# Two-layer token kernel: the first stage's preparation of a tile moved from one to three tiles ahead

## The chip, the cores and the metric

One core of a Trainium2 chip runs the kernel; all inputs and outputs lie in its memory. The metric is the device time of one execution in microseconds (us), lower is better.

## The reference, cut to what matters

`x` is [32, 64, 1024] in float32, 2048 tokens of 1024 features (32 batches of 64 channels).

```python
x = x + ffn0(cond0(x, cond_128))      # first stage
x = x + ffn1(cond1(x, cond_128))      # second stage
# cond0: a weighted mix of eight 64x64 kernels for each batch
att = softmax(mlp(cond_128))                      # [32, 8]
y = einsum('boi,bih->boh', einsum('bk,koi->boi', att, weight), x) + (att @ bias_k)[:, :, None]
# ffn0: eight experts that scale inputs and outputs of one product with the signs of W
routing = softmax(y @ gate_w.T)                   # [2048, 8]
out = (y * (routing @ in_scale)) @ sign(W).T * (routing @ out_scale) + bias
# cond1: grouped convolution over the features; ffn1: dense product plus gated low-rank experts
```

## The kernel before, in words

The 2048 tokens are 16 tiles of 128 tokens (two batches each), in pairs: tile t is written `(i, p)` with t = 2i + p. Two stages follow one another. The first computes x1 = x + ffn0(cond0(x)) tile by tile and stores x1 in a scratch tensor; the second reads x1 back and computes the output. The change is in the first stage, its start and its hand-over to the second.

Five engines have their programs written out by hand, each in its own order, tied by semaphores.

**TensorE** (PE). For tile t of the first stage it makes `product_y` (L375 to L384: the 128x128 block-diagonal mixing matrix `agg` of two batches against x, eight float32 matmuls, 16 records, L382), `product_logits` (L386 to L393: eight matmuls with y as the stationary operand and eight moving columns, 16 records, L391), `turn_routing` (a transpose, L397), `product_scales` (L399 to L412: eight 32-row matmuls and two 32-row ones of 512 columns, L405 and L411), and the signed product `ffn0_step`, 32 matmuls of 128x512 (L429) into two banks. A period (`period0`, L442) is the signed product of one tile with the preparation of the next one set in: y ahead of it, logits at step 12, the transpose at 20, scales at 26.

**VectorE** (DVE) adds the mixing bias to y (L748), makes the next mixing matrix (`mix_kernels`, L719 and L724), takes part in the softmax (L755, L757, L762), scales y to u (`scale_in`, L769), makes the low part of u (`take_rest`, L776), and scales the product (`scale_out`, L784). **ScalarE** (ACT) takes the signs at the start (L586), makes the exponentials (L593), spreads and rounds the routing (L598, L604), rounds u (L609), copies the out-scales from the bank to `os_sb` (`copy_out_scale`, L620, which waits for POOL to be done with the tile before), and rounds one chunk of the second stage's weights per pair (L624).

**GpSimd** (POOL) makes x + bias in one of two buffers `resid` (`add_bias0`, L891), reading x from `xs`; then x1 from it, half by half (`make_x1`, L899); and once per pair the low part of a chunk of weights (`rest_of_stage`, L903). Its order for a pair: x1 of tile (i,0), a chunk, bias of (i+1,0), x1 of (i,1), bias of (i+1,1). The bias add waits until x1 of the tile two before is stored, since it writes the same buffer.

**SyncE** (SP) issues nearly all transfers, in program order and waiting in line: for a pair x of the next pair (L222), the bias row of the tile (L227), the store of x1 (L263), a chunk of weights (L230). At the hand-over it issues the 16 loads of the second stage's first two tiles (`load_raw`, L303) behind the store of tile 13. In the second stage it stores an output tile, waits for the landing, and reloads x1 into the same buffer (L327, L318); POOL adds a bias to it (L931).

The second stage is 16 periods of L491 (its dense products), L473 (the convolution) and L519. Its first product waits for the low parts of u's successor z (L776), and for `rest_of_stage` of the eighth chunk.

## Time and profile before

| | us |
|---|---|
| median of 3 runs | 585.76 (585.52 to 588.63) |
| the profiled execution's own time | 585.94 |
| its span | 584.2 |
| PE busy | 569.8 (98%) |
| DVE busy | 232.6 (40%) |
| POOL busy | 148.1 (25%) |
| ACT busy | 118.9 (20%) |
| first stage's steady periods, from the span's start | 38.4 to 204.2 |
| second stage begins | 215.0 |

A timeline row gives start and duration in us, the engine, the line of the kernel, the operation, what it writes and reads, how many instructions are merged in it, and in brackets the idle time before it and what ended that. In a row of PE the duration is from the first start to the last end, and a matmul of 0.4 us overlaps the next one, so a group's cost is read from start to start, or from the chain of waits, whose pieces do not overlap. A row of a transfer gives its issue; the time from issue to landing stands in the rows of its line. A name such as `work` stands for both `resid` and `os_sb`, which are parts of it.

### The profile page before, as it was taken

What the parts mean: (1) busy time and instruction counts of PE and PEld (TensorE: products, weight loads), DVE (VectorE), ACT (ScalarE), POOL (GpSimd) and SP (SyncE); (2) the same over time, 40 slices, a digit from 0 to 9 for tenths busy, and PEclk for the clock granted to TensorE, in tenths of its full rate; (3) what the DMA queues carried; (4) which work ended last, traced back from release to release, by engine and by line L of the source; (5) the groups of instructions that cost most, each with busy time, mean ns of one, the idle gap of its engine ahead of it and who ended that gap; (6) DMA issues with size and microseconds to landing.
All of it is one profiled execution on the core that took longest, in us unless ns stands there. A gap on an engine that the chain in (4) does not pass through costs nothing.

```text
span 584.2 us, 9131 instructions
## 1 busy us (share of the span) xinstructions
PE 569.8 (98%) x3381; PEld 502.3 (86%) x3381; DVE 232.6 (40%) x446; ACT 118.9 (20%) x271; POOL 148.1 (25%) x79
## 2 busy tenths in 40 slices
PE   4799999999999999999999999999999999999997
PEld 3688888888888899989989889899899898898996
DVE  3675677557765555221232232222312322222121
ACT  4732333324233341011111011011110110100100
POOL 0425636555456456101011011011010110110100
PEclk9889999999999999999999999999999999999999
DMA  8905324443253664303203123033032130230100
GB/s 327 356 34 162 117 78 132 135 119 117 76 175 100 158 165 123 111 3 113 90 24 112 45 67 112 33 79 103 9 112 75 37 112 36 76 111 8 67 37 36
DMA packets 36175, 58.16 MB, mean 100 GB/s; under 512 B 4097, under 2 KB 24385, under 8 KB 36161
## 3 DMA queue, kind: packets, MB, share of 16 engines
q1 hardware_dynamic: 36016, 57.70, 31.9%
q10 hardware_dynamic: 144, 0.26, 0.1%
q8 instruction: 10, 0.16, 0.1%
q14 instruction: 5, 0.03, 0.0%
HBM read 41.15 MB, written 16.79 MB: 99 GB/s over the span
## 4 chain that ended last, share of the span: by engine, by line
PE 94%; DVE 0%; issue 0%
PE bank L491 49%; PE bank L429 21%; PE bank L473 10%; PE bank L391 4%; PE bank L382 4%; PE bank L519 4%; PE bank L405 1%; PE bank L397 0%; PE bank L512 0%; PE bank L411 0%; DVE work L748 0%; DVE work L874 0%
## 5 line engine op out<-in xcount | busy, mean ns | idle before, releaser
L491 PE MATMUL bank<-early,parts 128*128 128x320 f32 (+1 forms) x1152 | 206.5, 337 | 0.0
L491 PEld LDWEIGHTS bank<-early,parts 128*128 128x128 f32 x1152 | 184.7, 188 | 15.7
L429 PE MATMUL bank<-late,parts 128*128 128x512 f32 x512 | 134.5, 411 | 1.5 <-ACT parts L609 1.5
L429 PEld LDWEIGHTS bank<-late,parts 128*128 128x128 f32 x512 | 93.5, 193 | 21.9 <-ACT parts L609 1.9
L931 POOL TENSOR_TENSOR work<-work,bias_bc 128x1024 f32<-128x1024 f32 x16 | 38.7, 2424 | 286.5 <-DMA work<-x_scratch 286.5
L491 PE MATMUL bank<-late,parts 128*128 128x512 f32 x384 | 94.2, 394 | 0.0
L491 PEld LDWEIGHTS bank<-late,parts 128*128 128x128 f32 x384 | 70.9, 188 | 16.1
L473 PE MATMUL bank<-band,raw 128*128 128x128 f32 x512 | 59.7, 275 | 0.0
L473 PEld LDWEIGHTS bank<-band,raw 128*128 128x128 f32 x512 | 59.0, 192 | 0.1
L609 ACT ACTIVATE parts<-work 128x512 fp32r<-128x512 f32 x64 | 39.8, 632 | 80.3 <-DVE work L823 43.0
L899 POOL TENSOR_TENSOR work<-work 128x512 f32<-128x512 f32 x32 | 41.3, 1291 | 52.5 <-DVE work L784 52.5
L776 DVE TENSOR_TENSOR parts<-work,parts 128x512 fp32r<-128x512 f32 x64 | 46.8, 753 | 12.2 <-ACT parts L609 10.6
L891 POOL TENSOR_TENSOR work<-xs,bias_bc 128x1024 f32<-128x1024 f32 x16 | 38.7, 2424 | 45.3 <-DMA x_scratch<-work 23.1
L845 DVE TENSOR_TENSOR qk<-bank,qk 128x256 f32<-128x256 f32 x16 | 6.8, 424 | 100.5 <-ACT qk L666 100.5
L864 DVE TENSOR_TENSOR wh_t<-bank,wh_t 128x128 fp32r<-128x128 f32 x16 | 4.7, 292 | 95.0 <-ACT wh_t L674 95.0
L874 DVE TENSOR_TENSOR work<-bank,work 128x512 f32<-128x512 f32 x32 | 22.1, 692 | 50.7 <-PE bank L519 50.7
L382 PEld LDWEIGHTS bank<-agg,xs 128*128 128x128 f32 x256 | 32.5, 200 | 1.4 <-issue 0.2
L391 PEld LDWEIGHTS bank<-cst,work 128*128 128x128 f32 x256 | 31.4, 194 | 2.0 <-issue 0.9
L382 PE MATMUL bank<-agg,xs 128*128 128x128 f32 x256 | 33.0, 285 | 0.0
L391 PE MATMUL bank<-cst,work 128*128 128x8 f32 x256 | 30.1, 253 | 0.5 <-DVE work L748 0.5
L664 ACT ACTIVATE qk<-bank 128x64 f32<-128x64 f32 x16 | 3.6, 225 | 119.0 <-PE bank L491 119.0
L519 PE MATMUL bank<-lora,wh_t 128*128 128x512 f32 x96 | 27.6, 396 | 0.0
(88 smaller groups left out, 344.4 us busy)
## 6 DMA issues: line engine op xcount, KB each, us to landing
xs<-in_x SPq DMA_DIRECT2D x16, 512.0 KB, 3.9
x_scratch<-work SPq DMA_DIRECT2D x16, 512.0 KB, 3.0
raw<-x_scratch SPq DMA_DIRECT2D x128, 64.0 KB, 3.0
work<-x_scratch SPq DMA_DIRECT2D x16, 512.0 KB, 3.6
out_tokens<-work SPq DMA_DIRECT2D x15, 512.0 KB, 2.7
stage<-in_wearly SPq DMA_DIRECT2D x8, 576.0 KB, 3.8
row_bc<-token_rows_scratch SPq DMA_DIRECT2D x30, 64.0 KB, 3.6
work<-in_wsign SPq DMA_DIRECT2D x3, 512.0 KB, 11.3
```

The costliest lines, as they stand in the source:

```text
L382: last = mm(bank[h][:, c * P:(c + 1) * P], xs[:, p, at:at + P], agg[:, p, :], start=True, stop=True)
L391: last = mm(bank[2][:, 0:E], y_t[:, c, :], cst[:, C_GATE + c * E:C_GATE + (c + 1) * E], start=(c == 0), stop=(c == L8 - 1))
L429: last = mm(bank[4 + h][:, :], parts[:, p, a, c, :], signs[:, c, h * HALF:(h + 1) * HALF], start=(k % 16 == 0), stop=(k % 16 == 15))
L473: last = mm(bank[n // 4][:, (n % 4) * P:(n % 4 + 1) * P], raw[:, p, n, s:s + P], band[:, s * GROUPS + n % 4, :], start=(s == 0), stop=(s = ...
L491: return mm(dst, parts[:, p, a, c, :], w(b, c), start=(k == 0), stop=(close and k == 23))
L519: last = mm(o[h][:, :], wh_t[:, a, :], lora[:, b, h * HALF:(h + 1) * HALF], start=False, stop=(k == 2))
L609: do(cols(parts[:, p, 0], h), cols(y_t, h), ACT.Copy).then_inc(done, 1)
L776: v.tensor_tensor(cols(parts[:, p, 1], h), cols(y_t, h), cols(parts[:, p, 0], h).bitcast(F32), ALU.subtract).then_inc(done, 1)
L874: v.tensor_tensor(o, bank[4 + 2 * p + h][:, :], o, ALU.add).then_inc(out_ready, 1)
L891: g.tensor_tensor(resid[:, p, :], xs[:, p, :], bias_bc[:, :], ALU.add).then_inc(xb_ready, 2)
L899: g.tensor_tensor(resid[:, p, cols], os_sb[:, cols], resid[:, p, cols], ALU.add).then_inc(x1_ready, 1)
L931: g.tensor_tensor(resid[:, p, :], resid[:, p, :], bias_bc[:, :], ALU.add).then_inc(resid_ready, 1)
```

## The change

The first stage becomes a pipeline three tiles deep. In the period of tile t (`i, p`), `one` is tile t+1, `two` t+2, `three` t+3.

- `product_y` uses 64x64 quarters of the array: 32 matmuls of 64 rows, 64 stationary columns and 64 moving columns, on `agg` without its zero blocks. It serves tile t+3.
- `product_logits` has the gate weights, padded to 32 columns, as the stationary operand, and y as the moving one, in four column groups of the array; ACT copies the four partial sums (`copy_logits`), and a matmul `sum_logits` with a selection matrix adds them. Logits serve tile t+2; the sum stands at step 26.
- The transpose of the routing stands at step 7. Logits, y and scales stand together at step 18, the scales of tile t+1 last; these wait for the out-scale copies of tile t.
- y has two buffers of its own; `xs` is let go as soon as y is made, so x is loaded three tiles ahead. x is loaded a second time, straight into `resid`, by `load_again`, and POOL adds the bias in place. `load_again` of tile t+1 is issued by SP behind the store of tile t-1 and its landing (`replace_x1`).
- POOL's order becomes, for each tile t: first half of x1(t), bias of t+1, in every second tile a chunk, second half of x1(t).
- `mix_kernels` needs one reduction of 128 partitions in place of two of 64.
- At the start the constants come in three parts, the signs' loads and roundings are in another order, and the first stage's periods 0 and 1 are written out; at the hand-over SP issues `load_raw` of the second stage's first two tiles ahead of the store of tile 13 and the reload for tile 15.

The diff, cut to its core (indentation shortened):

```diff
-LOGITS_AT, TURN_AT, SCALES_AT, CONV0_AT = 12, 20, 26, 8
-SIGNS_FIRST = 6
+TURN_AT, BLOCK_AT, SUM_AT, CONV0_AT = 7, 18, 26, 8
+SIGNS_FIRST = 4
...
-        work = sb("work", [P, 4, H])
+        y_t = sb("y_t", [P, 2, L8, P])
+        work = sb("work", [P, 3, H])
         xs = sb("xs", [P, 2, H])
         raw = sb("raw", [P, 2, NBG, NB])
...
-        agg = sb("agg", [P, 2, P])
+        agg = sb("agg", [P, 2, S])
...
+  def load_next(i, p, biased):
+      sp.wait_ge(y_biased, biased)
+      load_x(i, p)
+      load_row(aggb_row, i, p, aggb_loaded)
+  def load_again(i, p):
+      sp.dma_start(resid[:, p, :], tile_rows(x, 2 * i + p)).then_inc(x_again_loaded[p], 16)
+  sp.wait_ge(rows_stored, 16)
+  load_next(1, 0, 2)
+  for p in range(2):
+      sp.wait_ge(signs_ready, 7 + p)
+      load_again(0, p)
   sp.wait_ge(scale_ready, 1)
   sp.dma_start(bias_bc[:, :], bias0.broadcast_to([P, H])).then_inc(bias0_loaded, 16)
-  sp.wait_ge(tok_rows_ready, 2)
-  sp.dma_start(rows_dram.rearrange("a b s -> b a s"), tok_rows[:, :, :]).then_inc(rows_stored, 16)
+  load_next(1, 1, 4)
...
+  load_stage(1, bm, H)
   load_stage(0, wearly[:, 0, :], NW)
-  sp.wait_ge(signs_ready, 2)
-  load_stage(1, bm, H)
+  load_next(2, 0, 6)
   for k in range(2):
-      sp.wait_ge(signs_ready, 3 + k)
       sp.dma_start(late_raw[:, k, :], late_pairs[k]).then_inc(late_loaded[k], 16)
-  sp.wait_ge(signs_ready, 6)
   sp.dma_start(band[:, :, :].rearrange("p a n -> p (a n)"), toep).then_inc(band_loaded, 16)
...
+  def store_x1(i, p):
+      sp.wait_ge(x1_ready, 4 * i + 2 * p + 2)
       sp.dma_start(tile_rows(x1_dram, 2 * i + p), resid[:, p, :]).then_inc(x1_stored[p], 16)
-  def load_next(i, p, both):
-      sp.wait_ge(xb_ready, both)
-      sp.wait_ge(y_biased, both)
-      load_x(i + 1, p)
-      load_row(aggb_row, i + 1, p, aggb_loaded)
-  with sp.Fori(0, PAIRS - 1) as i:
-      load_next(i, 0, 4 * i + 2)
-      store_x1(i, 0, 4 * i + 2)
-      load_next(i, 1, 4 * i + 4)
+  def replace_x1(i, p):
+      store_x1(i, p)
+      sp.wait_ge(x1_stored[p], 16 * (i + 1))
+      load_again(i + 1, p)
+  def next_chunk(i):
       sp.wait_ge(stage_hi[0], i + 1)
       sp.wait_ge(stage_lo[0], i + 1)
       load_stage(0, wearly[:, bass.ds(i + 1, 1), :].rearrange("p a n -> p (a n)"), NW)
-      store_x1(i, 1, 4 * i + 4)
+  with sp.Fori(0, PAIRS - 3) as i:
+      load_next(i + 2, 1, 4 * i + 8)
+      replace_x1(i, 0)
+      next_chunk(i)
+      load_next(i + 3, 0, 4 * i + 10)
+      replace_x1(i, 1)
+  late_i, last = PAIRS - 3, PAIRS - 1
+  load_next(last, 1, 4 * late_i + 8)
+  replace_x1(late_i, 0)
+  next_chunk(late_i)
+  replace_x1(late_i, 1)
...
+  sp.wait_ge(y_done, 2 * TILES - 2)
+  sp.dma_start(xs[:, 0, :], late_pairs[3]).then_inc(late_loaded[3], 16)
   for p in range(2):
       sp.wait_ge(y_biased, 4 * last + 2 * p + 2)
       load_row(ctx_row, 0, p, ctx_loaded)
+  replace_x1(last - 1, 0)
+  next_chunk(last - 1)
...
   load_raw(0, 0)
   load_raw(0, 1)
+  replace_x1(last - 1, 1)
   sp.wait_ge(xb_ready, 2 * TILES)
   sp.dma_start(bias_bc[:, :], bias1.broadcast_to([P, H])).then_inc(bias1_loaded, 16)
-  sp.dma_start(xs[:, 0, :], late_pairs[3]).then_inc(late_loaded[3], 16)
-  store_x1(last, 0, 4 * last + 2)
-  store_x1(last, 1, 4 * last + 4)
+  store_x1(last, 0)
+  store_x1(last, 1)
...
   def product_y(i, p):
-      pe.wait_ge(x_loaded[p], 16 * (i + 1))
-      pe.wait_ge(agg_ready, 4 * i + 2 * p + 2)
-      for h in range(2):
-          for c in range(4):
-              at = (4 * h + c) * P
-              last = mm(bank[h][:, c * P:(c + 1) * P], xs[:, p, at:at + P],
-                        agg[:, p, :], start=True, stop=True)
-          last.then_inc(y_done, 1)
-  def product_logits(i, p):
       for c in range(L8):
-          if c % 4 == 0:
-              pe.wait_ge(y_biased, 4 * i + 2 * p + 1 + c // 4)
-          last = mm(bank[2][:, 0:E], y_t[:, c, :], cst[:, C_GATE + c * E:C_GATE + (c + 1) * E],
-                    start=(c == 0), stop=(c == L8 - 1))
-      last.then_inc(logits_done, 1)
-  def turn_routing(i, p):
+          for b in range(2):
+              for g in range(2):
+                  at = c * P + g * S
+                  rows = slice(b * S, (b + 1) * S)
+                  made = mm(bank[b][g * S:(g + 1) * S, c * S:(c + 1) * S], xs[rows, p, at:at + S],
+                            agg[rows, p, :], start=True, stop=True)
+              if c == L8 - 1:
+                  made.then_inc(y_done, 1)
+  def product_logits(i, p, first_tile=False):
+      pe.wait_ge(y_biased, 4 * i + 2 * p + 2)
+      if not first_tile:
+          pe.wait_ge(gate_exp, 2 * i + p)
+      for c in range(L8):
+          at = slice(EP * (c % 4), EP * (c % 4) + EP)
+          made = mm(bank[2][at, 0:P], cst[:, C_GATE + c * EP:C_GATE + (c + 1) * EP], y_t[:, p, c, :],
+                    start=(c < 4), stop=(c >= 4))
+      made.then_inc(logits_made, 1)
+  def sum_logits(i, p, first_tile=False):
+      pe.wait_ge(logits_copied, 2 * i + p + 1)
+      if not first_tile:
+          pe.wait_ge(u_ready, 4 * i + 2 * p - 1)
+      mm(bank[2][:, 0:E], logits_t[:, :], cst[:, C_SEL:C_SEL + E], start=True, stop=True).then_inc(logits_done, 1)
...
+  def product_scales(i, p, first_tile=False, copied=1):
       pe.wait_ge(routing_split, 2 * i + p + 1)
+      pe.wait_ge(logits_copied, 2 * i + p + copied)
+      if not first_tile:
+          pe.wait_ge(out_scale_ready, 4 * i + 2 * p)
...
+  def period0(i, p, one, two=None, three=None):
       for k in range(32):
-          if k == LOGITS_AT:
-              pe.wait_ge(u_ready, 4 * i + 2 * p + 2)
-              product_logits(ni, q)
           if k == TURN_AT:
-              turn_routing(ni, q)
-          if k == SCALES_AT:
-              pe.wait_ge(out_scale_ready, 4 * i + 2 * p + 2)
-              product_scales(ni, q)
-          ffn0_step(i, p, k, first_tile)
-  period0(0, 0, 0, 1, True)
-  period0(0, 1, 1, 0)
-  with pe.Fori(1, PAIRS - 1) as i:
-      period0(i, 0, i, 1)
-      period0(i, 1, i + 1, 0)
+              turn_routing(*one)
+          if k == BLOCK_AT:
+              if three:
+                  inputs_of_y(*three)
+              if two:
+                  product_logits(*two)
+              if three:
+                  product_y(*three)
+              product_scales(*one, copied=2 if two else 1)
+          if k == SUM_AT and two:
+              sum_logits(*two)
+          ffn0_step(i, p, k)
+  for k in range(32):
+      if k == 6:
+          pe.wait_ge(u_ready, 1)
+          product_logits(0, 1)
+      if k == 10:
+          inputs_of_y(1, 0)
+          sum_logits(0, 1)
+          product_y(1, 0)
+      if k == 16:
+          turn_routing(0, 1)
+      if k == 22:
+          inputs_of_y(1, 1)
+          product_logits(1, 0)
+          product_y(1, 1)
+          product_scales(0, 1, copied=2)
+      if k == 28:
+          sum_logits(1, 0)
+      ffn0_step(0, 0, k, True)
+  period0(0, 1, (1, 0), (1, 1), (2, 0))
+  with pe.Fori(1, PAIRS - 2) as i:
+      period0(i, 0, (i, 1), (i + 1, 0), (i + 1, 1))
+      period0(i, 1, (i + 1, 0), (i + 1, 1), (i + 2, 0))
   last_i = PAIRS - 1
-  period0(last_i, 0, last_i, 1)
+  period0(last_i - 1, 0, (last_i - 1, 1), (last_i, 0), (last_i, 1))
+  period0(last_i - 1, 1, (last_i, 0), (last_i, 1))
+  period0(last_i, 0, (last_i, 1))
...
+  def copy_logits(i, p):
+      act.wait_ge(logits_made, 2 * i + p + 1)
+      do(logits_t[:, :], bank[2][:, 0:P], ACT.Copy).then_inc(logits_copied, 1)
...
+  def period0(i, p, one, two=None, chunk=None):
+      if one:
+          round_routing(*one)
+      copy_out_scale(i, p, 1)
+      if chunk is not None:
+          round_stage(0, NW, (chunk + 1) * 16, early[:, 0, bass.ds(chunk, 1), :].rearrange("p a n -> p (a n)"))
+      if two:
+          copy_logits(*two)
+      if one:
+          round_u(*one)
+      if two:
+          gate_exps(*two)
+          spread_routing(*two)
+      if one:
+          copy_out_scale(*one, 0)
...
+  period0(last, 0, (last, 1))
+  period0(last, 1, None, None, last)
...
-      for h in range(2):
-          rows = slice(h * S, (h + 1) * S)
-          v.tensor_reduce(agg[rows, p, rows], weighted[rows, :, :], AX.X, ALU.add).then_inc(agg_ready, 1)
+      v.tensor_reduce(agg[:, p, :], weighted[:, :, :], AX.X, ALU.add).then_inc(agg_ready, 1)
...
+  add_mix_bias(0, 0, True)
+  dve.wait_ge(scale_hi, 1)
+  v.scalar_tensor_tensor(scale_w[:, :], bias_bc[:, 0:HALF], cst[:, C_SLO:C_SLO + 1], scale_w[:, :].bitcast(F32),
+                         ALU.mult, ALU.add).then_inc(scale_ready, 1)
+  mix_kernels(0, 1)
+  route_max(0, 0)
+  route_sum(0, 0)
   split_routing(0, 0)
   scale_in(0, 0)
-  take_rest(0, 0, u_hi, u_lo, by_block)
-  period0(0, 0, 0, 1, first=True)
-  period0(0, 1, 1, 0)
-  with dve.Fori(1, PAIRS - 1) as i:
-      period0(i, 0, i, 1)
-      period0(i, 1, i + 1, 0)
+  rest_of_u(0, 0, 0)
+  add_mix_bias(0, 1, True)
+  rest_of_u(0, 0, 1)
+  mix_kernels(1, 0)
+  route_max(0, 1)
+  route_sum(0, 1)
+  mix_kernels(1, 1)
+  add_mix_bias(1, 0)
+  split_routing(0, 1)
+  scale_out(0, 0, 0)
+  scale_in(0, 1)
+  rest_of_u(0, 1, 0)
+  route_max(1, 0)
+  rest_of_u(0, 1, 1)
+  route_sum(1, 0)
+  add_mix_bias(1, 1)
+  mix_kernels(2, 0)
...
+  def period0(i, p, before, one, two=None, three=None, four=None):
+      scale_out(*before, 1)
+      split_routing(*one)
+      if four:
+          mix_kernels(*four)
+      scale_out(i, p, 0)
+      scale_in(*one)
+      rest_of_u(*one, 0)
+      if two:
+          route_max(*two)
+      rest_of_u(*one, 1)
+      if two:
+          route_sum(*two)
+      if three:
+          add_mix_bias(*three)
+  period0(0, 1, (0, 0), (1, 0), (1, 1), (2, 0), (2, 1))
+  with dve.Fori(1, PAIRS - 2) as i:
+      period0(i, 0, (i - 1, 1), (i, 1), (i + 1, 0), (i + 1, 1), (i + 2, 0))
+      period0(i, 1, (i, 0), (i + 1, 0), (i + 1, 1), (i + 2, 0), (i + 2, 1))
   last = PAIRS - 1
-  period0(last, 0, last, 1, False)
+  period0(last - 1, 0, (last - 2, 1), (last - 1, 1), (last, 0), (last, 1))
+  period0(last - 1, 1, (last - 1, 0), (last, 0), (last, 1))
+  period0(last, 0, (last - 1, 1), (last, 1))
+  scale_out(last, 0, 1)
...
-  def add_bias0(i, p, first_tiles=False):
-      pool.wait_ge(x_loaded[p], 16 * (i + 1))
-      if not first_tiles:
-          pool.wait_ge(x1_stored[p], 16 * i)
-      g.tensor_tensor(resid[:, p, :], xs[:, p, :], bias_bc[:, :], ALU.add).then_inc(xb_ready, 2)
-  def make_x1(i, p):
+  def add_bias0(i, p):
+      pool.wait_ge(x_again_loaded[p], 16 * (i + 1))
+      g.tensor_tensor(resid[:, p, :], resid[:, p, :], bias_bc[:, :], ALU.add).then_inc(xb_ready, 2)
+  def make_x1(i, p, h):
       pool.wait_ge(xb_ready, 4 * i + 2 * p + 2)
-      for h in range(2):
-          pool.wait_ge(scaled, 4 * i + 2 * p + h + 1)
-          cols = slice(h * HALF, (h + 1) * HALF)
-          g.tensor_tensor(resid[:, p, cols], os_sb[:, cols], resid[:, p, cols], ALU.add).then_inc(x1_ready, 1)
+      pool.wait_ge(scaled, 4 * i + 2 * p + h + 1)
+      cols = slice(h * HALF, (h + 1) * HALF)
+      g.tensor_tensor(resid[:, p, cols], os_sb[:, cols], resid[:, p, cols], ALU.add).then_inc(x1_ready, 1)
...
-  pool.wait_ge(signs_ready, L8)
+  pool.wait_ge(u_lo, 2)
   pool.wait_ge(bias0_loaded, 16)
-  add_bias0(0, 0, True)
-  add_bias0(0, 1, True)
+  add_bias0(0, 0)
+  def period0(i, p, one, chunk=None):
+      make_x1(i, p, 0)
+      if one:
+          add_bias0(*one)
+      if chunk is not None:
+          hi, lo = (early[:, a, bass.ds(chunk, 1), :].rearrange("p a n -> p (a n)") for a in range(2))
+          rest_of_stage(0, NW, chunk + 1, lo, hi)
+      make_x1(i, p, 1)
+  period0(0, 0, (0, 1))
   rest_of_stage(1, H, 1, lora[:, 1, :], lora[:, 0, :])
   with pool.Fori(0, PAIRS - 1) as i:
-      make_x1(i, 0)
-      chunk = [early[:, a, bass.ds(i, 1), :].rearrange("p a n -> p (a n)") for a in range(2)]
-      rest_of_stage(0, NW, i + 1, chunk[1], chunk[0])
-      add_bias0(i + 1, 0)
-      make_x1(i, 1)
-      add_bias0(i + 1, 1)
+      period0(i, 1, (i + 1, 0), i)
+      period0(i + 1, 0, (i + 1, 1))
   last = PAIRS - 1
-  make_x1(last, 0)
-  rest_of_stage(0, NW, L8, early[:, 1, L8 - 1, :], early[:, 0, L8 - 1, :])
-  make_x1(last, 1)
+  period0(last, 1, None, last)
```

## Rows read from the trace of the kernel before

**Rows 1.** The page: busy time, share of the span and instructions of each engine.

```profile
PE 569.8 (98%) x3381; PEld 502.3 (86%) x3381; DVE 232.6 (40%) x446; ACT 118.9 (20%) x271; POOL 148.1 (25%) x79
```

**Rows 2.** Chain of waits, start, us, what: tile 14's period and the hand-over.

```profile
192.33 1.78 PE bank L382 x16
...
196.85 1.69 PE bank L391 x16
...
202.58 3.56 PE bank L429 x14
206.14 3.57 PE bank L473 x32
209.71 5.46 PE bank L429 x24
```

**Rows 3.** Timeline of PE, the scale products of one period.

```profile
71.64 0.33 PE L405 MATMUL bank<-routing_t,scale_w 32*128 32x128 f32 x2
71.65 0.50 PE L411 MATMUL bank<-scale_w,routing_t 32*128 32x512 f32 x2
```

**Rows 4.** Timeline of POOL, two tiles of the first stage.

```profile
90.80 2.65 POOL L903 TENSOR_TENSOR early<-stage,early 128x1152 f32 x1 [1.96 <-ACT early L624]
93.42 2.39 POOL L891 TENSOR_TENSOR work<-xs,bias_bc 128x1024 f32<-128x1024 f32 x1
...
99.38 1.30 POOL L899 TENSOR_TENSOR work<-work 128x512 f32<-128x512 f32 x1 [2.33 <-DVE work L784]
103.90 2.40 POOL L891 TENSOR_TENSOR work<-xs,bias_bc 128x1024 f32<-128x1024 f32 x1 [3.22 <-DMA x_scratch<-work]
```

**Rows 5.** Timeline around a second-stage reload: DVE, SP and POOL.

```profile
307.55 0.69 DVE L874 TENSOR_TENSOR work<-bank,work 128x512 f32<-128x512 f32 x1 [2.67 <-PE bank L519]
308.43 0.37 SPq L327 DMA_DIRECT2D out_tokens<-work  x1
...
311.11 0.33 SPq L318 DMA_DIRECT2D work<-x_scratch  x1
...
314.50 2.36 POOL L931 TENSOR_TENSOR work<-work,bias_bc 128x1024 f32<-128x1024 f32 x1 [20.09 <-DMA work<-x_scratch]
```

**Rows 6.** Page, transfers by kind: count, KB each, median us from issue to landing.

```profile
xs<-in_x SPq DMA_DIRECT2D x16, 512.0 KB, 3.9
x_scratch<-work SPq DMA_DIRECT2D x16, 512.0 KB, 3.0
...
work<-x_scratch SPq DMA_DIRECT2D x16, 512.0 KB, 3.6
```

**Rows 7.** The store's line L263, over all 16, min/median/max.

```profile
DMA to landing us min/median/max: 2.9/3.0/7.3
```

**Rows 8.** Busy times by stretch: the start at half clock, then the steady periods.

```profile
24.20:27.90 3.70, 3.70 (x10) 2.71 (x11) 3.70 (x2) 2.31 (x4) 3.70 (x3) 0.54 0.97 343
...
38.40:204.20 165.80, 165.80 (x1051) 141.04 (x1050) 106.35 (x194) 54.30 (x120) 87.74 (x49) 1.00 0.40 123
```

**Rows 9.** Timeline of SP, the hand-over to the second stage.

```profile
197.88 7.47 SPq L303 DMA_DIRECT2D raw<-x_scratch  x16
...
205.87 0.43 SPq L313 DMA_DIRECT2D xs<-in_wlate  x1
207.28 10.38 SPq L263 DMA_DIRECT2D x_scratch<-work  x2
```

**Rows 10.** Timeline of DVE at the start.

```profile
22.64 1.29 DVE L769 TENSOR_TENSOR work<-bank,work 128x512 f32<-128x512 f32 x2 [0.75 <-PE bank L405]
24.09 4.21 DVE L776 TENSOR_TENSOR parts<-work,parts 128x512 fp32r<-128x512 f32 x2 [0.16 <-ACT parts L609]
```

**Rows 11.** Timeline of ACT, the hand-over to the second stage.

```profile
207.34 0.60 ACT L620 ACTIVATE work<-bank 128x512 f32<-128x512 f32 x1 [2.29 <-POOL work L899]
207.84 1.16 ACT L624 ACTIVATE early<-stage 128x1152 fp32r<-128x1152 f32 x1
208.89 0.62 ACT L609 ACTIVATE parts<-work 128x512 fp32r<-128x512 f32 x1
```

223 lines of the change are left out of this document (117 added, 106 removed).

## The prediction

> **What bounds the kernel now.** I read the page first, for the shares: PE is busy 98% of the span and no other engine over 40% [rows 1]. Then the chain of waits in order of time, which shows who sets the pace: in the first stage it is PE alone, in periods of 11.845 us, from 38.4 us (tile 1) to 204.2, all of it busy at full clock [rows 8]; the last full one, tile 14's, starts at 192.33, and the next product of its tile 15 runs on to 215.17, where the second stage begins [rows 2]. Last I read POOL, SP and the transfers, which are not on the chain now, because the change re-orders them and makes them wait on one another in a new way.
>
> **PE's part.** A period holds y for 1.78 us and logits for 1.69 [rows 2]; 16 records each, 0.111 us per record. After, y has 64 records of half the columns. If the four quarters of the array work side by side, that is 16 x 0.056 = 0.9 us; if none do, 64 x 0.056 = 3.6. Logits: 16 records of 128 moving columns in four column groups, 4 x 0.111 = 0.45 side by side, 1.78 one by one; the sum adds 2 x 0.111 = 0.22. The nearest row for overlap is the scale products, four matmuls of different row groups that start within 0.01 us [rows 3]; for column groups no row stands. I take overlap for both. No row prices a change of the array's shape by itself; I allow 0.15 us for each of the two more, between nothing and 0.3. PE's period would be 11.85 - 3.47 + 0.9 + 0.45 + 0.22 + 0.3 = 10.25 us, 1.6 less.
>
> **The new chain through POOL.** x + bias was made from `xs`, which had been loaded long before. Now x is loaded again into `resid`, and only after the store of the tile two before has landed there. Follow one round, from the end of the second half of x1(t-1): SP wakes and issues the store; it lands; SP wakes and issues the reload for tile t+1; it lands; POOL adds the bias for t+1; in every second tile it makes the low part of a chunk; and only then, in its program order, the second half of x1(t). That is a loop from one tile to the next, whatever PE does. Its terms:
> - Store, landing, reload, landing. The second stage does exactly this: DVE ends at 308.24, POOL starts at 314.50, 6.26 us [rows 5]. The store there goes to the output; to the scratch tensor it costs more, POOL's end at 100.68 to its restart on the landing at 103.90 is 3.22 [rows 4], against 2.87 (to the reload's issue) there. With 3.39 for reload and landing and 0.1 for SP's wake I take 6.7. Lower end 6.3; upper end 7.1, from a median of 3.9 for a load of x with another transfer beside it [rows 6].
> - Bias 2.40, second half 1.29 [rows 4]: 3.69.
> - Chunk 2.65 in every second tile [rows 4].
> - In the odd tiles SP is held until that chunk is done, 1.29 us before the x1 ends, and then issues the chunk load (576 KB), x (512 KB) and a row ahead of the store. SP's own issues run to about 0.6 us past x1's end, and the 1.1 MB need 3.3 us at the 343 GB/s of the crowded start [rows 8], of which some 1.1 are left when the store is queued. I take 1.7 for both; lower end 0.6; upper end 4.3, since a store behind two 512 KB loads took 7.3 in place of 3.0 us [rows 7, 9]. Five tiles have it, one more 0.7.
>
> So a pair takes 2 x (6.7 + 3.69) + 2.65 + 1.7 = 25.1 us, 12.6 per tile, against 11.85 now and the 10.25 that PE could do. PE is tied to it: the scales of t+1 wait for ACT's out-scale copy of t, which waits for the second half of x1(t-1). PE waits some 2 us a period at step 18. The routing chain (max, exponential, transpose) was moved a period ahead and has slack of several us; the queues of DVE and ACT are in that wait's shadow, as what stands behind the copy on ACT (chunk rounding 1.16, logits copy about 0.3) delays the scales to 2.3 us after x1, and x1(t)'s own product is ready by about 7, before POOL needs it at 9.1.
>
> One more load on that loop has no row in steady state: a DVE instruction with both inputs in SBUF beside a POOL one. At the start two roundings' rests took 4.21 us in place of 1.3 [rows 10], with POOL at work. That is DVE held up; the loop suffers only if POOL is. I take nothing for it, and keep 0.8 a tile (the mixing product) as its upper end. The Trainium skill (SBUF — State Buffer, section on the two separate sides) says that such pairs lock each other out for a whole instruction, whoever is first; by that rule DVE's mixing product could hold POOL once a tile and the sum would be up to 10 us higher. The trace agrees that the lock exists (4.21 us), and shows no case where POOL lost.
>
> **Start.** The signed product of tile 0 starts as before: the same chain of short steps leads to u at 22.64 [rows 10]. But the second half of tile 0's scale-out moved on DVE behind the mixing work of later tiles: from 22.64 it has 22 operations of 512 columns at 0.7 and six small ones, 16.4 us, so 39.0, and x1(0) would end at 40.3 if DVE never waited. It waits for the scales of tile 1, which stand at step 22 of a half-clocked PE; I take 43.5, with 46 as upper end.
>
> **To tile 13.** 13 rounds of 10.39 are 135.1, seven chunks 18.6, the crowding 5 x 1.7 + 0.7 = 9.2: x1(13) is done at 43.5 + 162.9 = 206.4.
>
> **Hand-over.** Ahead of the store of tile 13 SP now has the chunk load and 16 issues of raw loads, 7.47 us [rows 9]. SP is let go 1.3 before x1(13) ends, so the store is issued 7.2 us after it. Then landing 3.2, reload 3.6: 14.0; bias and half of x1(14) 3.7: 17.7. ACT's copy 0.60, the last chunk's rounding 1.16, both roundings of z 1.25 [rows 11]: 20.7. DVE: last rest of z and scale-out of tile 15, 0.7 each: 22.1. POOL: first half of x1(15), 1.29, then the last chunk, 2.65: 26.1 us. Without that chunk the second stage may not begin. PE alone would be there after 15.5 us (1.3 to the end of the scales, 14 + 32 steps of 0.228 and the convolution's 3.57, all [rows 2]), so it idles some 10 us. The second stage begins at 206.4 + 26.1 = 232.5 in place of 215.2: 17.3 later. After a wait PE restarts at half clock (1.2 of 2.4 GHz): in 24.20 to 27.90 ten records took 3.7 us at a mean clock of 0.54 after a wait of PE [rows 8], and ten at full speed take 2.3 (5.46 for 24 in [rows 2]), so 1.5 are lost; with a second spell like it, 3. I take 1.7.
>
> The second stage's instructions and their order are unchanged. **Sum:** 585.94 + 17.3 + 1.7 = 604.9 for the profiled execution, which stands 0.2 from the median: 605.
>
> **Rivals.**
> - PE sets the pace (faster). It needs a loop under 10.25 us: 6.7 would have to be 5.2 or less, after the 3.69 and the mean chunk of 1.33. Against it: no store landed under 2.9 us and the measured round trip is 6.26 [rows 5, 7]. If it holds, 13 periods and a half at 1.6 less: 585.9 - 22 = 564. The Trainium skill (TensorE: Matmul & The Clock Gate, Part 1) gives a floor of about 25 ns from start to start for small matmuls; y would then be an estimated 1.6 in place of 0.9 and this rival 573. Rows 3's starts, four within 0.01 us, speak against it. Chance 0.07.
> - The loop binds, but mildly (no change): round trip 6.2, no crowding, x1(0) at 40.3. Then x1(13) ends at 40.3 + 13 x 9.89 + 18.6 = 187.5, and with the same hand-over the second stage begins at 213.6: 585.9 - 1.6 + 1.7 = 586. Chance 0.06.
> - Column groups don't overlap (slower, by PE): y 3.6 and logits 1.78 in each period, 14.3 us per tile, over the loop's 12.6. Then 14 x 2.5 = 35 later: 621, and the hand-over's gap closes partly. It decides from a PE period above 12.6. Chance 0.07.
> - The forecast, 0.80. Its own range: round trip, crowding and x1(0) at their low ends take off 5, 6 and 3, giving 592 with a small allowance; crowding, lock and clock at the high ends together would add 13, 10 and 2, of which I take about three quarters: 623.
>
> **Numbers.** 605; range 591 to 623, which holds nearly all of the forecast and of the third rival. A difference under 0.5% (2.9 us) can't be told from none. Faster 0.07, same 0.06, slower 0.87.
>
> **What would show it.** Right: chain of waits with POOL's bias add waiting for the reload, store and load of x in turn, periods of 12 to 13 us alternating short and long, PE idle at step 18 behind the out-scale copy; a gap of several us on PE ahead of the second stage; half clock after it. Wrong: PE busy without gaps in the first stage at 10.3 us a tile, or a POOL that waits for DVE rather than for the reload. If the new y and logits stretches last over 3.6 and 1.7 us, the third rival holds. A hand-over gap under 3 us would break my sum's second part.

## The result and the profile after

The changed kernel takes 620.41 us (median of 4 runs, 618.89 to 621.86) against 585.64 (585.13 to 588.63): a ratio of 1.058, 95% interval [1.055, 1.062]. It is slower, as forecast, and within the range of 591 to 623, but near its upper end, 15 us over the forecast of 605. The profiled execution took 618.89 us, its span is 616.9.

The page after, busy times, as in [rows 1], and the forty slices of PE and its clock:

```profile
PE 559.0 (91%) x4181; PEld 483.5 (78%) x4181; DVE 226.3 (37%) x429; ACT 121.8 (20%) x287; POOL 150.7 (24%) x79
...
PE   4697887979779882999999999999999999999997
...
PEclk9799788979797997999999999999999999999999
```

PE is busy 11 us less, in a span 33 us longer. The waits are in the first sixteen slices (15.4 us each), and its clock falls there again and again. So read what it waits for. The chain of waits of the changed kernel, one round of two tiles in the first stage (start, us, what):

```profile
89.83 5.78 DMA x_scratch<-work
...
95.78 3.24 DMA work<-in_x
...
99.49 1.97 issue
101.46 1.28 POOL work L1031
...
102.91 2.64 DMA x_scratch<-work
...
105.72 3.30 DMA work<-in_x
...
109.29 2.22 issue
111.50 3.15 POOL early L1035
```

Not one piece is PE's. Store, reload, POOL's bias add (printed as issue after its start), in the second tile the chunk, the second half of x1, and the store again: the ring of the prediction. In a tile with a chunk the printed chain goes from the chunk to the next store through the three issues of SP that the chunk lets go; they end with the second half of x1, within 0.3 us. POOL's timeline over the same round; L1024 is the bias add, L1035 the chunk, L1031 the halves of x1:

```profile
85.20 2.68 POOL L1035 TENSOR_TENSOR early<-stage,early 128x1152 f32 x1
87.83 1.73 POOL L1031 TENSOR_TENSOR work<-work 128x512 f32<-128x512 f32 x1
89.83 1.27 POOL L1031 TENSOR_TENSOR work<-work 128x512 f32<-128x512 f32 x1 [0.26 <-DVE work L888]
99.15 2.36 POOL L1024 TENSOR_TENSOR work<-work,bias_bc 128x1024 f32<-128x1024 f32 x1 [8.06 <-DMA work<-in_x]
101.46 2.49 POOL L1031 TENSOR_TENSOR work<-work 128x512 f32<-128x512 f32 x2
109.16 2.39 POOL L1024 TENSOR_TENSOR work<-work,bias_bc 128x1024 f32<-128x1024 f32 x1 [5.20 <-DMA work<-in_x]
111.50 3.14 POOL L1035 TENSOR_TENSOR early<-stage,early 128x1152 f32 x1
```

L1031 at 87.83 and the first part of the merged row at 101.46 are second halves. From the end of a second half (89.56) to the next bias add is 9.59 us when a chunk and x stand ahead of the store in the queue, and 6.42 us (102.74 to 109.16) when they don't. SP's timeline shows the three issues ahead of it:

```profile
88.09 0.33 SPq L235 DMA_DIRECT2D stage<-in_wearly  x1
88.71 0.33 SPq L227 DMA_DIRECT2D xs<-in_x  x1
89.22 0.33 SPq L232 DMA_DIRECT2D row_bc<-token_rows_scratch  x1
89.83 0.35 SPq L286 DMA_DIRECT2D x_scratch<-work  x1
95.78 0.33 SPq L265 DMA_DIRECT2D work<-in_x  x1
```

PE in that period: logits (L433), y (L420), then the wait at step 18, and the scales (L462):

```profile
98.96 0.64 PE L433 MATMUL bank<-y_t,cst 128*32 128x128 f32 x16
99.53 1.16 PE L420 MATMUL bank<-agg,xs 64*64 64x64 f32 x64
104.74 0.47 PE L462 MATMUL bank<-routing_t,scale_w 32*128 32x128 f32 x2 [4.04 <-ACT logits_t L672]
```

The new products are as cheap as taken: logits 0.57 us and y about 1.0 from start to start, for 1.69 and 1.78 of [rows 2]. All quarters and column groups work side by side. What they save PE then spends waiting, 4.04 us here. The wait is printed against the logits copy on ACT, but that one stands behind the out-scale copy, which waits for POOL. The granted clock falls to half (1.2 GHz) during this wait, by 103.0, 1.7 us ahead of the restart, and stays there until some 5 us behind it. The row's columns are those of [rows 8], the clock (0.51) is the third from the end:

```profile
103.20:109.70 6.50, 4.96 (x21) 4.10 (x22) 1.98 (x3) 2.66 (x5) 1.30 (x2) 0.51 0.43 161
```

Last the hand-over, PE's timeline, and SP's, which answer to [rows 2, 9]:

```profile
229.41 5.70 PE L486 MATMUL bank<-late,parts 128*128 128x512 f32 x24
246.61 3.59 PE L570 MATMUL bank<-early,parts 128*128 128x320 f32 x14 [11.50 <-POOL early L1035]
```

```profile
218.54 8.48 SPq L335 DMA_DIRECT2D raw<-x_scratch  x16
227.06 0.43 SPq L286 DMA_DIRECT2D x_scratch<-work  x1
230.27 0.35 SPq L265 DMA_DIRECT2D work<-in_x  x1
```

The store of tile 13 is issued 7.8 us after its x1 is done (219.23), behind the issues of 16 raw loads, and PE stands 11.5 us until POOL has made the last chunk.

Where the 32.7 us of span come from, from the end of x1 of tile 0 and of tile 13 (POOL's timeline) and the start of the second stage:

| stretch | before | after | more |
|---|---|---|---|
| to the end of x1(0) | 41.4 | 46.6 | 5.2 |
| 13 rounds to x1(13) | 154.0 (11.85 each) | 172.6 (13.28) | 18.6 |
| x1(13) to the second stage | 19.6 | 27.4 | 7.8 |
| second stage | 369.2 | 370.3 | 1.1 |

### The profile page after: what moved, and what is told of

The parts are those of the page before. It is cut to its first block, busy times and chain, and to the rows that moved or that the text cites. A ratio compares the mean times of both kernels' runs of the same rounds, so it can differ in the third digit from the quotient of the medians.

```text
span 616.9 us, 10810 instructions
## 1 busy us (share of the span) xinstructions
PE 559.0 (91%) x4181; PEld 483.5 (78%) x4181; DVE 226.3 (37%) x429; ACT 121.8 (20%) x287; POOL 150.7 (24%) x79
## 4 chain that ended last, share of the span: by engine, by line
PE 64%; DMA 15%; issue 7%; POOL 6%; SPq 3%; ACT 2%; DVE 2%; POOLq 0%; ACTq 0%; DVEq 0%
PE bank L570 47%; PE bank L552 9%; DMA x_scratch<-work 8%; DMA work<-in_x 7%; POOL early L1035 4%; PE bank L598 4%; PE bank L486 2%; POOL work L1031 2%; SPq L335 1%; PE bank L420 1%; ACT early L706 1%; ACT late L662 0%; DVE work L888 0%; PE bank L433 0%; DVE parts L880 0%
## 5 line engine op out<-in xcount | busy, mean ns | idle before, releaser
L570 PE MATMUL bank<-early,parts 128*128 128x320 f32 (+1 forms) x1152 | 207.9, 339 | 11.5 <-POOL early L1035 11.5
L486 PE MATMUL bank<-late,parts 128*128 128x512 f32 x512 | 141.2, 431 | 1.5 <-ACT parts L692 1.5
L486 PEld LDWEIGHTS bank<-late,parts 128*128 128x128 f32 x512 | 101.7, 207 | 24.8 <-ACT parts L692 1.6
L1066 POOL TENSOR_TENSOR work<-work,bias_bc 128x1024 f32<-128x1024 f32 x16 | 37.7, 2357 | 289.2 <-DMA work<-x_scratch 289.2
L570 PE MATMUL bank<-late,parts 128*128 128x512 f32 x384 | 93.9, 393 | 0.0
L570 PEld LDWEIGHTS bank<-late,parts 128*128 128x128 f32 x384 | 70.9, 188 | 15.8
L1024 POOL TENSOR_TENSOR work<-work,bias_bc 128x1024 f32<-128x1024 f32 x16 | 38.1, 2382 | 127.1 <-DMA work<-in_x 94.5
L880 DVE TENSOR_TENSOR parts<-y_t,parts 128x512 fp32r<-128x512 f32 x64 | 49.2, 771 | 21.6 <-ACT parts L692 20.2
L692 ACT ACTIVATE parts<-y_t 128x512 fp32r<-128x512 f32 x64 | 39.6, 631 | 70.6 <-DVE y_t L959 42.0
L1031 POOL TENSOR_TENSOR work<-work 128x512 f32<-128x512 f32 x32 | 43.7, 1376 | 13.1 <-DVE work L888 13.1
L873 DVE TENSOR_TENSOR y_t<-bank,y_t 128x512 f32<-128x512 f32 x32 | 20.6, 686 | 51.7 <-PE bank L462 51.7
L462 PE MATMUL bank<-routing_t,scale_w 32*128 32x128 f32 x128 | 12.9, 327 | 29.1 <-ACT logits_t L672 24.5
L462 PEld LDWEIGHTS bank<-routing_t,scale_w 32*128 32x128 f32 x128 | 10.6, 226 | 31.2 <-issue 25.8
L702 ACT ACTIVATE work<-bank 128x512 f32<-128x512 f32 x32 | 18.7, 588 | 72.1 <-POOL work L1031 72.1
```

Source lines behind the costliest of these rows:

```text
L462: made = mm(bank[2 + h][:, c * P:(c + 1) * P], scale_w[rows, c * P:(c + 1) * P], routing_t[rows, :], start=True, stop=True)
L486: last = mm(bank[4 + h][:, :], parts[:, p, a, c, :], signs[:, c, h * HALF:(h + 1) * HALF], start=(k % 16 == 0), stop=(k % 16 == 15))
L570: return mm(dst, parts[:, p, a, c, :], w(b, c), start=(k == 0), stop=(close and k == 23))
L692: do(cols(parts[:, p, 0], h), cols(src, h), ACT.Copy).then_inc(done, 1)
L880: v.tensor_tensor(cols(parts[:, p, 1], h), cols(src, h), cols(parts[:, p, 0], h).bitcast(F32), ALU.subtract).then_inc(done, 1)
L1024: g.tensor_tensor(resid[:, p, :], resid[:, p, :], bias_bc[:, :], ALU.add).then_inc(xb_ready, 2)
```

## The experiments

The time of each version is a median, its ratio is to the kernel before measured beside it; that kernel's medians were 586.0 to 587.9 us in the four sets of runs, so a difference of 2 us between two sets says nothing. Rounds and start are read from one profiled execution each.

**The chunk out of the ring.** On POOL alone, in the changed kernel:

```diff
             def period0(i, p, one, chunk=None):
                 make_x1(i, p, 0)
-                if one:
-                    add_bias0(*one)
                 if chunk is not None:
...
                     rest_of_stage(0, NW, chunk + 1, lo, hi)
+                if one:
+                    add_bias0(*one)
                 make_x1(i, p, 1)
```

> The changed kernel with POOL's chunk (2.7 to 3.1 us in every second tile) ahead of the bias add, so that it runs while the reload is in flight. POOL loop theory (store, reload, bias, second half of x1 in a ring): the chunk leaves the ring, seven times about 3 us, and the loads behind it are issued earlier, so the pair falls from 26.7 us to about 23 and the time to 592 to 600. Rival (TensorE sets the pace, by its new small matmuls or its half clock, and POOL only follows): no change, 618 to 623.

Measured 582.14 us, ratio to the kernel before 0.994 [0.991, 0.997]: two lines of POOL's program exchanged give back 38 us. That is more than I expected. A round is 10.66 us (x1(0) at 47.3, x1(13) at 185.9), which is 34 of the 38 us; the gap ahead of the second stage is 7.63 us for 11.50. Besides the chunk's own 3 us, the crowding went: SP is let go by the chunk while the reload is in flight, so chunk and x are under way long before the next store. The store's landing (min/median/max) in this kernel between 100 and 160 us:

```profile
DMA to landing us min/median/max: 2.6/2.7/3.0
```

against 5.78 and 2.64 in turn above. With PE's waits short, the half clock goes too: its mean over the 13 rounds is 0.99, where it was 0.89. The rival, that PE sets the pace, predicted no change and is out.

**x behind the store.** Only `load_next(i + 3, 0, ...)` moved behind `replace_x1(i, 1)` in SP's loop:

```diff
                 next_chunk(i)
-                load_next(i + 3, 0, 4 * i + 10)
                 replace_x1(i, 1)
+                load_next(i + 3, 0, 4 * i + 10)
```

> The changed kernel with the load of x for a tile ahead (512 KB) and its row moved behind the store and reload of the odd tile, five times. Crowding theory: that store took 5.3 to 5.8 us in place of 2.7 to 3 because 1.1 MB stood ahead of it; with only the chunk's 576 KB ahead it takes about 4, and the time falls by 5 to 10 us, to 610 to 615. Rival (it is the chunk load alone, or the x loads arrive too late for TensorE then): 618 or more.

611.95 us, ratio 1.043 [1.039, 1.047], 8.5 less than the changed kernel. x1(13) ends at 211.1 in place of 219.2. So x alone in the queue ahead costs 8.1 us, 1.6 in each of the five rounds that have it; the chunk has the rest of the crowding (the store lands in 3.85 us, between 5.8 and 2.6).

**Without the reload.** POOL adds the bias to itself and waits for the store only. This leaves x out of the first stage's residual sum:

```diff
-                pool.wait_ge(x_again_loaded[p], 16 * (i + 1))
-                g.tensor_tensor(resid[:, p, :], resid[:, p, :], bias_bc[:, :], ALU.add).then_inc(xb_ready, 2)
+                if wait:
+                    pool.wait_ge(x1_stored[p], 16 * i)
+                g.tensor_tensor(resid[:, p, :], bias_bc[:, :], bias_bc[:, :], ALU.add).then_inc(xb_ready, 2)
...
                 store_x1(i, p)
-                sp.wait_ge(x1_stored[p], 16 * (i + 1))
-                load_again(i + 1, p)
```

> The changed kernel without the second load of x: POOL's bias add reads the bias twice and waits only for the store of the tile two before; this leaves x out of the first stage's residual sum. POOL loop theory: the ring shrinks by the reload's 3.5 us and its crowding, to about 8.5 us a tile, under TensorE's own 10.3; the first stage runs at TensorE's pace, 10.2 to 10.6 us a tile, and the time is 570 to 585. Rival (TensorE's small matmuls or column groups cost more than they save): the first stage stays over 11.8 us a tile and the time over 600.

585.26 us, ratio 0.997 [0.994, 1.000], at the upper end of my range. A round is 10.91 us, 2.4 less than in the changed kernel, so the reload is on the ring. But that is longer than the 10.2 to 10.6 that I expected at PE's pace, and no shorter than in the first run, which has the reload. DVE's timeline shows a second cost; L877 is the low part of u:

```profile
116.94 1.88 DVE L877 TENSOR_TENSOR parts<-y_t,parts 128x512 fp32r<-128x512 f32 x1
...
118.81 3.06 DVE L877 TENSOR_TENSOR parts<-y_t,parts 128x512 fp32r<-128x512 f32 x1
```

with POOL's timeline beside it, the bias add and the chunk:

```profile
116.37 1.89 POOL L1022 TENSOR_TENSOR work<-bias_bc 128x1024 f32<-128x1024 f32 x1 [0.28 <-DMA x_scratch<-work]
118.22 3.10 POOL L1033 TENSOR_TENSOR early<-stage,early 128x1152 f32 x1
```

A DVE instruction of 0.69 us lasts until 0.55 us after the end of POOL's bias add, and the next one until 0.55 us after POOL's chunk (118.82 and 121.87, against POOL's ends at 118.26 and 121.32). All four read two operands from SBUF. Behind that part of u stand DVE's reciprocal and ACT's routing, and PE waits 1.71 us for these at its transpose, at 122.52.

**The store ahead of the raw loads**, at the hand-over:

```diff
+            store_x1(last - 1, 1)
             load_raw(0, 0)
+            sp.wait_ge(x1_stored[1], 16 * last)
+            load_again(last, 1)
             load_raw(0, 1)
-            replace_x1(last - 1, 1)
```

> The changed kernel with the store of tile 13 ahead of the 16 raw loads and its reload between the first eight and the last eight. Hand-over theory: the store no longer stands behind 7.5 us of issues, TensorE's gap ahead of the second stage falls from 11.5 us to about 4, the time to 611 to 615. Rival (the gap is set by ACT's and DVE's order, not by SP's): within 1 us of 620.

615.35 us, ratio 1.048 [1.045, 1.052], 5 less. The gap falls from 11.5 to 6.19 us, not to 4: the reload stands behind eight raw issues, 5.9 us behind the store, lands in 4.6 us, and PE's gap is still ended by the eighth chunk on POOL. The profiled execution is the fastest of its five, 611.56 us; its 13 rounds take 169.1 us for 172.6, with nothing changed in them. So two executions can differ by 3 us in the rounds for no reason in the kernel.

**y made twice.** Each 64x64 product twice, in the changed kernel, and the same in the mended one of the next run. This is the test of who sets the pace.

```diff
+                            for again in range(2):
-                            made = mm(bank[b][g * S:(g + 1) * S, c * S:(c + 1) * S], xs[rows, p, at:at + S],
-                                      agg[rows, p, :], start=True, stop=True)
+                                made = mm(bank[b][g * S:(g + 1) * S, c * S:(c + 1) * S], xs[rows, p, at:at + S],
+                                          agg[rows, p, :], start=True, stop=True)
```

> The changed kernel with each of the 64x64 mixing products made twice (same result): TensorE gets 0.93 us more work in each of 14 periods. Ring theory: TensorE waits over 4 us in a period for POOL's ring, so this is hidden but for the start and a few half-clock stretches: 619 to 625. Rival (TensorE sets the pace): 13 us more, or more than that at half clock, 633 to 645.

629.62 us, ratio 1.074 [1.069, 1.079]: 9 us more, between the two. The total alone would not decide it; the rounds do. x1(0) ends at 58.3 in place of 46.6, and from there the 13 rounds take 170.6 us, against 172.6 without the doubling. In each round 1.1 us of added PE work cost nothing that can be told from the spread. The 9 us come from the start, where the chain runs through PE. Up to the scales of tile 1 (48.67 for 38.47) some 4.5 us are the doubled products, and 5.7 more go to two pauses of PE for which the profile names no wait (printed as issue): 1.80 us at 38.5, and 4.55 us in the midst of the doubled y, where the changed kernel has 0.70. No run here shows what these pauses are.

**The hand-over mended.** Chunk out of the ring, the store's new place, and

```diff
-            period0(last, 0, (last, 1))
-            period0(last, 1, None, None, last)
+            period0(last, 0, (last, 1), None, last)
             act.wait_ge(ffn0_done, 2 * TILES - 2)
             round_parts(0, 0, z_t, z_biased, z_hi, by_token)
+            period0(last, 1, None)
```

on ACT (z of the second stage's first tile is rounded ahead of the last period), and on POOL the eighth chunk one tile earlier too.

> The first run (chunk ahead of the bias add) with the second run's order of SP at the hand-over, the eighth chunk rounded and subtracted one tile earlier, and z rounded by ACT ahead of the out-scale copy of tile 15's second half. Hand-over theory: nothing that the second stage's first product needs waits for the reload of tile 15 any more, so TensorE's gap of 7.6 us ahead of it closes and the restart at half clock with it: 572 to 576. Rival (the gap moves to another wait, the out-scales of tile 15 or the late weights): 579 or more.

574.82 us, ratio 0.980 [0.975, 0.985]. PE's timeline there, the signed product of tile 15 and the second stage behind it:

```profile
198.26 5.71 PE L487 MATMUL bank<-late,parts 128*128 128x512 f32 x24
203.81 7.20 PE L571 MATMUL bank<-early,parts 128*128 128x320 f32 x48
```

No wait between them. The gap, 7.6 us in the first run, is gone; ahead of it PE waits 0.87 us for raw loads, at 194.69. Three edits were made at once here, and no run parts them.

**y twice in the mended kernel.**

> The same doubling in the mended kernel of the first run of this set. There ring (about 10.6) and TensorE (about 10.3) are close, so with 0.93 us more TensorE sets the pace: 7 to 13 us over that kernel. Rival (the ring still leaves TensorE much idle there): under 3 us.

595.74 us, ratio 1.017 [1.011, 1.022]: 21 us more, well over my 13. Again the start takes 11.7 of it (x1(0) at 57.8 for 46.1), with the same two pauses, 1.82 and 4.28 us. The 13 rounds take 149.9 us for 140.9, 0.7 each. Here the added products are on the path. In the changed kernel the printed chain touches PE in two of the 13 rounds only, at 77.76 and 209.08, and not y. Here it runs through PE from one block at step 18 to the next in most rounds (L435 is the logits, L422 y, 106.49 to 117.69):

```profile
106.49 0.57 PE bank L435 x16
107.06 2.17 PE bank L422 x125
...
117.69 0.34 PE bank L435 x5
```

**The store in halves.** In the mended kernel each half of x1 is stored as soon as it is made.

```diff
             def store_x1(i, p):
-                sp.wait_ge(x1_ready, 4 * i + 2 * p + 2)
-                sp.dma_start(tile_rows(x1_dram, 2 * i + p), resid[:, p, :]).then_inc(x1_stored[p], 16)
+                for h in range(2):
+                    sp.wait_ge(x1_ready, 4 * i + 2 * p + h + 1)
+                    cols = slice(h * HALF, (h + 1) * HALF)
+                    sp.dma_start(tile_rows(x1_dram, 2 * i + p)[:, cols], resid[:, p, cols]).then_inc(x1_stored[p], 16)
```

> The same with each half of x1 stored as soon as it is made, so that only 256 KB stand between the second half and the reload. Ring theory: the ring of about 10.1 us a tile loses 0.5 to 0.8 us, and the first stage comes to TensorE's own 10.3 or so: 2 to 5 us less than the run without the split, 568 to 573. Rival (a transfer's time is mostly fixed, or POOL and DVE blocking each other is what is left): within 1 us of it.

575.86 us, ratio 0.981 [0.977, 0.986], against 574.82 with whole stores: no gain, as the rival had it. DVE's timeline in a round with a chunk shows why the bytes were not what was left:

```profile
118.47 1.87 DVE L883 TENSOR_TENSOR parts<-y_t,parts 128x512 fp32r<-128x512 f32 x1
...
120.34 2.81 DVE L883 TENSOR_TENSOR parts<-y_t,parts 128x512 fp32r<-128x512 f32 x1
```

Two instructions of 0.69 us last to 120.34 and 123.15, held by POOL's chunk (117.11 to 119.79) and its bias add (120.15 to 122.60), and POOL then waits 2.71 us for DVE's half of the scale-out.

**The chunk's rest on DVE** in place of POOL, and the same with the store in halves:

```diff
                 scale_out(i, p, 0)
+                if chunk is not None:
+                    dve.wait_ge(stage_hi[0], chunk + 1)
+                    hi, lo = (early[:, a, bass.ds(chunk, 1), :].rearrange("p a n -> p (a n)") for a in range(2))
+                    v.tensor_tensor(lo, stage[:, 0, 0:NW], hi.bitcast(F32), ALU.subtract).then_inc(stage_lo[0], 1)
                 scale_in(*one)
```

> The mended kernel (574.8) with the low part of the eight weight chunks made by DVE, in its gap between scale-out and scale-in, in place of POOL. Blocking theory: what keeps the mended kernel at 10.8 us a tile over TensorE's 10.1 is POOL's chunk beside DVE instructions with both inputs in SBUF, which hold each other up (a low part of u took 3.1 us in place of 0.7); with the chunk on DVE the first stage comes to 10.1 to 10.4 us a tile, the time to 566 to 571. Rival (the ring of store, reload, bias and half is what is left, the chunk lies in its shadow): 573 to 577. Second rival (DVE becomes the bound with 1.7 us more in every second tile): over 577.

572.41 us, ratio 0.975 [0.973, 0.978].

> The same with the stores of x1 by halves. If the ring of about 10.2 us is what is left then, it loses 0.5 us a tile and TensorE sets the pace: 2 to 4 us less than the run without the split. If TensorE sets the pace already, within 1 us of it.

571.77 us, ratio 0.974 [0.971, 0.976]. The first lies between its two expectations, 2.4 us under the mended kernel (10.59 us a round for 10.84), and the two intervals overlap. The second gains nothing that the intervals can tell from the first; its rounds are 10.36 us, but in an execution of 569.22 us, 2.6 under its median. So neither time by itself decides between the ring and the lock. The chain of the second is still the ring, now at its shortest, bias, half, store, reload:

```profile
117.26 1.70 POOL work L1031
...
119.63 1.31 POOL work L1038
...
121.09 2.51 DMA x_scratch<-work
...
123.81 3.56 DMA work<-in_x
...
127.50 1.59 POOL work L1031
```

All runs so far shortened the ring; none asked why it closes within one tile. There are two buffers, so the reload for tile t+1 might have two tiles' time. It has one because POOL's program puts the bias add of t+1, which waits for that reload, ahead of the second half of x1(t).

**The bias add last.** In the changed kernel, nothing else touched:

```diff
                 make_x1(i, p, 0)
-                if one:
-                    add_bias0(*one)
                 if chunk is not None:
...
                 make_x1(i, p, 1)
+                if one:
+                    add_bias0(*one)
```

> The changed kernel with one call moved on POOL: the bias add of tile t+1 behind the second half of x1(t), the chunk left where it is. The ring theory: the second half of x1 no longer waits for the reload, so store, reload, bias and half (up to 9.6 + 2.4 + 1.3 us and a chunk of 3.1) have two tiles' time in place of one and are under 2 x 10 us. PE then sets the pace: rounds of 10.0 to 10.6 us in place of 13.28, no wait for a reload on the chain of the steady part, and 571 to 579 us with a gap of 5 to 8 us left at the hand-over. Rival, that POOL's and DVE's own work and their holding one another set a pace behind the ring (10.91 us in the run without the reload): 583 us or more. Rival, that the order was no cause and the transfers alone set the pace: 610 to 620.

570.09 us, ratio 0.971 [0.968, 0.975]: one call moved takes off 50 us, a us more than my range allowed; the hand-over's gap is 3.6 us and not 5 to 8. Both rivals are out: with two tiles' time the transfers set no pace, and POOL's and DVE's own work sets none above PE's, though the lock is still there (a bias add takes 2.85 us here for 2.39). x1(0) ends at 46.8, x1(13) at 178.0: 10.09 us a round. From 60 to 170 us the chain has no wait in it, only PE's periods of 10.13:

```profile
98.25 0.57 PE bank L433 x16
98.82 1.09 PE bank L420 x64
...
108.38 0.57 PE bank L433 x16
```

POOL's timeline there has the reload, the chunk and all else of the ring, but where the bias add of the changed kernel waited 5.20 and 8.06 us for the reload, it now follows the second half at once, and POOL waits for DVE, and so for PE:

```profile
105.84 1.29 POOL L1031 TENSOR_TENSOR work<-work 128x512 f32<-128x512 f32 x1 [3.38 <-DVE work L888]
107.09 2.85 POOL L1024 TENSOR_TENSOR work<-work,bias_bc 128x1024 f32<-128x1024 f32 x1
110.09 1.28 POOL L1031 TENSOR_TENSOR work<-work 128x512 f32<-128x512 f32 x1 [0.16 <-POOL work L1024]
111.34 2.67 POOL L1035 TENSOR_TENSOR early<-stage,early 128x1152 f32 x1
```

**The same move in the best kernel so far.**

> The same move in the kernel with the chunk's rest on DVE, the halved store and the mended hand-over (571.77 us, 10.36 us a round, its chain still bias, half, store, reload). If that ring is all that holds PE there, rounds fall to PE's own 9.9 to 10.1 us, and the time to 566 to 569. If DVE's work in its order holds PE as well, no change: 571 to 573.

566.46 us, ratio 0.964 [0.961, 0.967]. Rounds of 10.07 us (x1(0) at 47.9, x1(13) at 178.8), and the second stage starts at 195.56 behind the signed product with no gap. This version beats both kernels. What it gains on the kernel before is what the change's cheaper products give: 13 rounds of 10.07 in place of 11.85 are 23 us. The start is 6.5 us longer and the hand-over 2.9 shorter, so the second stage begins 19.6 us sooner (195.56 for [rows 2]'s 215.17).

## Why the prediction was right, and where its sizes were off

The mechanism was right: the loop through POOL, closed by the bias add's place "in its program order", sets the pace, PE is tied to it at step 18, and the hand-over waits for the last chunk. That moving the bias add alone opens the loop and gives 570 shows it; that y made twice costs the changed kernel's rounds nothing shows PE is not the bound. The sum was 14 us short of the profiled execution (604.9 for 618.89), and the errors are in these terms:

- **PE's part.** Right. Logits 0.57 for 0.45 + 0.15, y 1.0 to 1.1 for 0.9 and the change of shape. The period was put at 10.25 and is 10.13 where PE is free. The Trainium skill (TensorE: Matmul & The Clock Gate, Part 1) gives some 25 ns from start to start as a floor; 64 records in 1.09 us are 17 ns each, so the trace disagrees, and y at the 1.6 us that the prediction estimated by it would have made the free period 10.6.
- **The round trip, 6.7 taken**: 6.42 us measured in the round shown where nothing is ahead of the store, 5.95 to 6.34 in the other four. With 6.42 for the crowded rounds too, this gave 4.7 us back.
- **The crowding, 1.7 taken: this is the term that was mis-sized.** 9.59 - 6.42 = 3.2 us in the odd rounds. I let the 1.1 MB ahead drain at 343 GB/s and took what was left; the store landed 5.8 us after its issue in place of 2.6. It lies inside the bounds of 0.6 to 4.3. In the five odd rounds it was 3.0 to 3.5 us, 16.2 in all for 8.5, in the sixth 1.4 for 0.7, and two rounds at the beginning had 2.0 and 0.7 that the sum left out. That is 11.1 us more than taken; with the round trip's 4.7 less and POOL's 3.4 more (the next point) it makes the 9.7 us by which the rounds' 172.6 exceeded the 162.9.
- **The lock between DVE and POOL, nothing taken, 0.8 a tile as the upper end.** Wrong as a choice: five of the seven chunks take 3.1 us in place of 2.65, and five second halves 1.73 for 1.29, 4.6 us in all. Instructions of POOL that follow one another overlap by some 0.05 us, so 3.4 are left in the rounds. The Trainium skill (SBUF — State Buffer, section on the two separate sides) says that the pair lock each other out whoever is first, and the trace now agrees in both directions: a DVE instruction of 0.69 us lasts 3.06 behind POOL's chunk (the run without the reload), and POOL's chunk at 111.50 lasts 3.14 when DVE's L880, begun at 109.86, runs on into it. The trace of the kernel before did show a case where POOL lost, against what the prediction says: beside the 4.21 us of [rows 10] its two bias adds took 5.16 us, for 2.39 each in [rows 4]. POOL's row of the kernel before, then DVE's of the changed kernel:

```profile
22.59 5.16 POOL L891 TENSOR_TENSOR work<-xs,bias_bc 128x1024 f32<-128x1024 f32 x2 [22.14 <-ACT late L586]
...
109.86 2.23 DVE L880 TENSOR_TENSOR parts<-y_t,parts 128x512 fp32r<-128x512 f32 x1
```

- **Start, 43.5 taken**: 46.6, over the upper end of 46. The step that failed is that the start is "as before": DVE begins to scale u at 24.47, not at 22.64, which is 1.8 of the 3.1 us. Then it waits 3.33 us for the scales of tile 1, and the chain from 25.9 to 39.2 is PE's, with a pause of 0.70 us in it that names no wait. That the start is 58.3 with y made twice shows that PE is on that path.
- **Hand-over, 26.1 taken**: 27.4. The store is issued 7.8 us after x1(13) for 7.2, and the chunk takes 3.59 us beside DVE for 2.65. With the store ahead of the raw loads, an earlier chunk and an earlier rounding of z no gap is left, which shows the causes together and not one by one.
- **Clock, 1.7 taken**: 1.1 in the second stage. The half clock around the long waits in the first stage had no term. PE has slack there; no run shows what it costs by itself.

The rival in which the loop binds mildly, at 586, had the round trip right (6.2) and failed on the crowding and the start. The rival in which column groups don't overlap is out: logits take 0.57 us and not 1.78. The rival of PE's pace, put at 564, is what the last two runs are (570.1 and 566.5): its price was about right, and its condition (a round trip of 5.2 us) was not the only way to it.

## What to carry to other kernels

When a load is made to wait for a store into the same buffer, write down the ring of waits and count over how many tiles it closes; an in-order engine that takes the dependent step one place too early halves that number, whatever the buffers. Move that step behind the last one that the other buffer needs before shortening any transfer: here one call moved was worth 50 us, and all the other edits together 49 (620.4 to 571.8). Price a transfer on a ring with what is queued ahead of it at that moment, not by its median.

## What the runs showed of the hardware that I had not expected

- A 512 KB store issued right behind a 576 KB and a 512 KB load landed in 5.8 us, and in 2.6 us when nothing was ahead (5.78 and 2.64 in the pair shown, 5.6 to 5.9 and 2.6 in the three behind it).
- A DVE instruction with two SBUF operands lasted 3.06 us in place of 0.69 beside a POOL one, in all four cases shown until 0.55 us after POOL's end; POOL's half of x1 took 1.73 in place of 1.28, its last chunk 3.59 in place of 2.68.
- 64x64 float32 products of all four quarters side by side: 64 records in 1.09 us; 16 logits records in four column groups: 0.57 us.
- In each of PE's five waits of 3.5 to 4.1 us in the changed kernel's rounds its clock fell to half (1.2 GHz), and it came back 5 to 7 us after the restart; a wait of 2.19 us cost a shorter stretch, waits of 1.97 and 2.48 us none. The mean over the rounds was 0.89. With one wait of 2.78 us and the others under 1, as in the run with the chunk ahead of the bias add, it was 0.99.
- PE paused for 0.70 us in the straight-line start of the changed kernel, and for 1.80 and 4.55 us with y made twice, with no wait that the profile names.
